# Attention layers: inverse sums applied to the weighted values of a head group instead of to the probabilities

## The chip, the core and the metric

The kernel runs on one core of a Trainium2 chip. Its engines are TensorE (PE; PEld is its weight load), VectorE (DVE), ScalarE (ACT), GpSimd (POOL) and SyncE (SP), which issues DMAs. The metric is the device time in microseconds of one execution, as the median of several runs.

## The reference

Four layers in a row on x of 4 x 512 x 512, all in float32. Layer 0 is attention with 16 heads of 32, normalized queries and keys, and an MLP; layer 1 is attention with a sparse causal mask, 16 heads of 32 and 4 key heads; layer 2 is attention with 8 heads of 64 on one key head, and a gated MLP; layer 3 is a set of small experts. What the change touches is in all three attentions (layer 0 shown; x grows by the result times gamma1):

```python
scores = jnp.einsum('bhqd,bhkd->bhqk', qn, kn) + attn_bias
p = jax.nn.softmax(scores, axis=-1)
o = jnp.einsum('bhqk,bhkd->bhqd', p, v)
o = jnp.transpose(o, (0, 2, 1, 3)).reshape(Bs, Lx, Cx)
return o @ Wproj.T + bproj
```

## The kernel before

One function, `attention`, builds the three attention layers (tags l0a, l1a, l2a), each as a block in which every engine has its own program. The batches (4) are the outer loop. A batch is cut into head groups of four heads (`NG` = 4 groups in layers 0 and 1, 2 in layer 2; `NO` accumulators psO of 128 rows each, 1 or 2), a head group into four tiles of 128 queries (`NT`), and a query tile into its four heads. So a head group has 16 steps, one for each pair of query tile and head, a batch 64 (layer 2: 32), and a quarter of a head group is four steps. The order is written out by hand: `steps` gives each engine, for step n, the same list of side jobs.

For the tile of step n:

- TensorE computes its scores (`scores`, 128 queries by up to 512 keys; 128 or 198 in layer 1) two steps ahead in layer 0, one step ahead in layers 1 and 2, into one of `NS` = 3 banks (layer 2: 2).
- VectorE adds the mask and takes the minimum of the negated scores (`minima`, L1095), which writes the tile to `prob`.
- ScalarE takes the exponential and the row's sum (`exps`, L837; sums in `ssum`).
- After four tiles, behind the minimum of the next one, VectorE makes the four inverse sums in one reciprocal (`inverse_sums`, L1102, of 128x4), and GpSimd multiplies the four tiles with them (L1259 and L1261) and counts `p_done`.
- Six steps after its own step (`LAG`), TensorE transposes the tile (`transposes`, L673, one transpose for each 128 keys). ScalarE copies three of four to `PT`, VectorE the fourth (L1110).
- `weigh` (L695) multiplies four such tiles with the values, into `psO`, which gathers a whole head group transposed: row 32j + d (or 64j + d) is column d of head j, the free axis is the 512 queries. The last one of a group is in step 7 of the next.
- In step 7 ScalarE copies `psO` to the high part `oTh` (`o_copy`, L855), in step 8 VectorE makes the remainder `oTl` (`o_rest`, L1117). Both add the value bias in layer 0. The output projection (`out`, L588) of a batch runs in the next one, as four side jobs at the steps `OUT_AT`, each with a residual on VectorE.

The other side jobs of TensorE all write one of two banks `psA`, in turn: the query and key projections of layer 0 (steps 2, 4, 6 and 9), its value projections (7 and 8), transposes of the normalized rows, and from step 12 to 15 those of the next group's queries and keys. VectorE prepares the next group meanwhile (`prepare`): in layer 0 squares and sums (steps 1 and 2), three steps of an inverse square root on 128x32 (steps 3 to 5, the helper at L82, L84 and L86), the scaling (6), and the split into stacked parts (9, 11, 13 and 14); in layers 1 and 2 rotations and stacks.

In layer 0 GpSimd also adds the projected bias `bG` to the four residual tiles, one in each of the last four quarters of a batch (L1267). SP loads `G` and `bG` for a batch after the residuals of the one before.

Of the kernel before, what the change touches and what calls it, by code (L numbers as in the profile page):

```python
# [25 lines left out]
P = 128  # L26
# [234 lines left out]
def attention(nc, R, D, L, scale_g, shift_g):  # L261
# [28 lines left out]
    with ExitStack() as ctx:  # L290
# [38 lines left out]
        rinv = S.sb("rinv", [P, NP])  # L329
# [4 lines left out]
        if is0:  # L334
            qb = S.sb("qb", [P, C])
            G = S.sb("G", [P, C])
            bG = S.sb("bG", [P, C])
            nrm = S.sb("nrm", [P, 4, 4 * 8])
            sq = xn[:].rearrange("p r c -> p (r c)").rearrange("p (t w) -> p t w", w=QKW)
# [17 lines left out]
        if is2:  # L357
# [19 lines left out]
        s_done, min_done, exp_done, rinv_done, p_done = (  # L377
            S.sem(n) for n in ("s_done", "min_done", "exp_done", "rinv_done", "p_done"))
# [17 lines left out]
        OUT_AT = (9, 10, 11, 20) if is0 else (12, 13, 14, 15)  # L396
# [17 lines left out]
        def jobs(n, first, more):  # L414
# [3 lines left out]
            todo = []  # L418
            if hg < NG:
# [41 lines left out]
        def banked(first, more, last):  # L461

            n_, out = 0, []
# [15 lines left out]
        with nc.Block() as block:  # L479

            @block.sync
            def _(sp):
# [29 lines left out]
            def _(pe):  # L512
# [79 lines left out]
                def run(job, i, b, bn, bo):  # L592
# [72 lines left out]
                def transposes(b, m, first):  # L665
# [3 lines left out]
                    pe.wait_ge(p_done, b * NTILE + (m + 1))  # L669
# [6 lines left out]
                def weigh(b, u, first):  # L676
# [53 lines left out]
            def _(act):  # L730
# [118 lines left out]
                def o_copy(b, hg):  # L849

                    act.wait_ge(pv_done, b * U + (hg + 1) * NT)
                    for o in range(NO):
                        k = hg % NG * NO + o
                        bias = R.vb[:, k:k + 1] if is0 else R.zero[:]
                        act.activation(oTh[:, k, :], psO[o][:], ACT.Identity, bias=bias).then_inc(oh_done, 1)  # L855

                def batch(b, first, more):
                    for n, _, todo, m in steps(first, more):
# [8 lines left out]
                        if n % GS == LAG + 1 and n <= NTILE + LAG + 1 and not (first and n == LAG + 1):  # L867
# [34 lines left out]
            def _(v):  # L902
# [62 lines left out]
                if is0:  # L965
                    qk_tiles = (nrm[:, 1, :], nrm[:, 0, :], nrm[:, 2, :], nrm[:, 3, :].bitcast(I32))
# [132 lines left out]
                def inverse_sums(b, u):  # L1099
# [996 lines left out]
```

## Time and profile before

| | us |
|---|---|
| median of 3 runs | 2933.84 (2933.4 to 2935.29) |
| the profiled execution | 2936.59 |
| its span, first to last instruction | 2934.8 |
| TensorE busy | 2468.2 (84%) |
| VectorE busy | 1624.5 (55%) |
| ScalarE busy | 1207.7 (41%) |
| GpSimd busy | 907.7 (31%) |

The mean granted clock of TensorE over the span is 0.89 of full speed. The score loops of the attention layers begin at 101, 1243 and 1735 us of the span and end at 760, 1652 and 2088. An MLP stands between the first two, layer 2's MLP and the experts behind the last. Busy time is a sum over the engine's instructions and does not tell whether somebody waited for them.

### The profile page before, as it was taken

To read this page: it belongs to the slowest core of one execution; us is meant where nothing else is said; L and a number is where in the kernel's file an instruction comes from. 1 tells how busy PE (TensorE), PEld (TensorE's weight loads), DVE (VectorE), ACT (ScalarE), POOL (GpSimd) and SP (SyncE) were. 2 spreads that over 40 slices of the span, in tenths; PEclk is the share of its full clock that TensorE was granted. 3 is DMA by queue.
4 is the path that set the end of the run, shared out by engine and by line. 5 is a ranking of instruction groups with operands and counts; after the bars stand their busy time and mean duration, and the time that the engine had idled before them with its cause. 6 is when DMAs were issued, how large, how long until landed. Compare 5 with 4: busy or idle time off the path is not lost. (4 is left out here: it accounts for less than half of the span.)

```text
span 2934.8 us, 48110 instructions
## 1 busy us (share of the span) xinstructions
PE 2468.2 (84%) x15828; PEld 2016.5 (69%) x15828; DVE 1624.5 (55%) x4635; ACT 1207.7 (41%) x2980; POOL 907.7 (31%) x982
## 2 busy tenths in 40 slices
PE   5879789798589999688788758889789999996786
PEld 4767677677468888576656547767568888885565
DVE  2677766677664343465575466576453333333876
ACT  1565565556441111365665546555431111112442
POOL 0133333233366676232232213233211212120422
PEclk8899889799889999768778779989989999997898
DMA  5000000000200000100000000000100000001000
GB/s 205 23 1 2 9 2 9 1 2 9 75 27 18 26 29 0 70 30 1 2 1 1 2 33 1 1 0 1 44 22 22 35 31 21 0 0 47 1 29 29
DMA packets 15743, 63.12 MB, mean 22 GB/s; under 512 B 2588, under 2 KB 3356, under 8 KB 10548
## 3 DMA queue, kind: packets, MB, share of 16 engines
q1 hardware_dynamic: 15540, 60.59, 5.8%
q8 instruction: 105, 1.72, 0.2%
q14 instruction: 98, 0.80, 0.1%
HBM read 56.36 MB, written 4.23 MB: 21 GB/s over the span
## 5 line engine op out<-in xcount | busy, mean ns | idle before, releaser
L837 ACT ACTIVATE l0a_prob<-l0a_prob,l0a_nmin 128x512 f32<-128x512 f32 x256 | 185.7, 725 | 199.5 <-DVE l0a_nmin L1095 199.2
L1617 POOL TENSOR_TENSOR l2m_hidl<-l2m_hid,l2m_hidh 128x512 fp32r<-128x512 f32 x64 | 100.9, 1576 | 480.2 <-DVE l2m_hidh L1593 480.2
L1259 POOL TENSOR_TENSOR l0a_prob<-l0a_prob,l0a_rinv 128x512 f32<-128x512 f32 x64 | 66.6, 1040 | 533.1 <-DVE l0a_rinv L1102 533.1
L1485 ACT ACTIVATE l2m_gate<-l2m_psG 128x512 f32<-128x512 f32 x64 | 38.3, 598 | 452.0 <-PE l2m_psU L1426 452.0
L1588 DVE TENSOR_TENSOR l2m_hid<-l2m_gate,l2m_psU 128x512 f32<-128x512 f32 x64 | 44.0, 688 | 300.1 <-ACT l2m_gate L1485 300.1
L673 PE MATMUL l0a_psT<-res_ident,l0a_prob 128*128 128x128 f32 x1024 | 165.9, 287 | 11.8 <-ACT l0a_PT L847 11.7
L1095 DVE CUSTOM_DVE_ANT_0 l0a_prob<-l0a_psS,l0a_mask 128x512 f32<-128x512 f32 x256 | 173.2, 687 | 2.6 <-issue 1.6
L1636 POOL TENSOR_TENSOR res_X<-res_X,l0m_share 128x512 f32<-128x512 f32 x128 | 162.1, 1293 | 25.7 <-DVE l0m_share L1577 24.7
L535 PE MATMUL l0a_psA<-l0a_wh,l0a_hTh 128*128 128x128 f32 (+1 forms) x512 | 155.5, 304 | 11.2 <-DVE l0a_wl L1210 5.8
L651 PE MATMUL l0a_psS<-l0a_kT,l0a_qT 96*128 96x512 f32 x256 | 128.0, 502 | 43.2 <-DVE l0a_nmin L1095 28.3
L1489 ACT ACTIVATE l0m_hid<-l0m_psG,l0m_b1c 128x512 f32<-128x512 f32 x64 | 44.0, 690 | 287.5 <-PE l0m_psG L1426 284.3
L673 PEld LDWEIGHTS l0a_psT<-res_ident,l0a_prob 128*128 128x128 f32 x1024 | 133.6, 147 | 38.6 <-ACT l0a_PT L847 19.0
L535 PE MATMUL l0a_psA<-l0a_wl,l0a_hTh 128*128 128x128 f32 (+1 forms) x512 | 149.2, 291 | 0.0
L535 PE MATMUL l0a_psA<-l0a_wh,l0a_hTl 128*128 128x128 f32 (+1 forms) x512 | 148.8, 291 | 0.0
L1261 POOL TENSOR_SCALAR l0a_prob<-l0a_prob,l0a_rinv 128x512 f32<-128x512 f32 x192 | 145.2, 772 | 0.0
L673 PE MATMUL l1a_psT<-res_ident,l1a_prob 128*128 128x128 f32 x448 | 120.5, 351 | 29.1 <-ACT l1a_PT L847 26.3
L837 ACT ACTIVATE l1a_prob<-l1a_prob,l1a_nmin 128x198 f32<-128x198 f32 (+1 forms) x256 | 114.6, 449 | 68.7 <-DVE l1a_nmin L1095 67.7
L1259 POOL TENSOR_TENSOR l1a_prob<-l1a_prob,l1a_rinv 128x128 f32<-128x128 f32 (+1 forms) x64 | 32.3, 505 | 338.4 <-DVE l1a_rinv L1102 338.4
L1259 POOL TENSOR_TENSOR l2a_prob<-l2a_prob,l2a_rinv 128x512 f32<-128x512 f32 x32 | 33.7, 1054 | 324.6 <-DVE l2a_rinv L1102 324.6
L847 ACT ACTIVATE l0a_PT<-l0a_psT 128x512 f32<-128x512 f32 x192 | 113.1, 595 | 41.7 <-PE l0a_psO L695 28.2
L837 ACT ACTIVATE l2a_prob<-l2a_prob,l2a_nmin 128x512 f32<-128x512 f32 x128 | 92.6, 724 | 87.5 <-DVE l2a_nmin L1095 87.2
L1593 DVE CAST l0m_hidh<-l0m_hid 128x512 fp32r<-128x512 f32 x64 | 33.0, 515 | 160.9 <-ACT l0m_hid L1489 160.9
(390 smaller groups left out, 7875.3 us busy)
## 6 DMA issues: line engine op xcount, KB each, us to landing
l2m_stage<-in_l2m_w SPq DMA_DIRECT2D x8, 1536.0 KB, 6.6
l0m_stage<-in_l0m_w SPq DMA_DIRECT2D x8, 1024.0 KB, 4.8
cond_w<-in_wmod SPq DMA_DIRECT2D x6, 1024.0 KB, 5.9
res_X<-in_x SPq DMA_DIRECT2D x4, 1024.0 KB, 11.9
l0a_prob<-in_l0a_w SPq DMA_DIRECT2D x4, 1024.0 KB, 6.6
l1a_wmod<-in_wmod SPq DMA_DIRECT2D x4, 1024.0 KB, 5.4
out<-res_X SPq DMA_DIRECT2D x4, 1024.0 KB, 4.3
l_stage<-in_l_w SPq DMA_DIRECT2D x3, 1024.0 KB, 7.2
```

Source lines behind the costliest of these rows:

```text
L535: mm = pe.matmul(ps[:, c0:c0 + n], l[:, k, t * P:(t + 1) * P], cols(r, k), start=(k == 0 and i == 0), stop=(k == NK - 1 and i == 2))
L651: mm = pe.matmul(out, q, kT[:, j, 0:w], start=True, stop=True)
L673: mm = pe.transpose(psT[m % 2][:, c * P:(c + 1) * P], prob[:, m % NP, k0:k0 + P], R.ident[:])
L837: act.activation(prob[:, n % NP, 0:w], src[:, 0:w], ACT.Exp, bias=nmin[:, n % NP:n % NP + 1], scale=-1.0, accum_out=ssum[:, n % NP:n % NP ...
L847: act.activation(PT[:, j, 0:w], psT[m % 2][:, 0:w], ACT.Copy).then_inc(pT_act, 1)
L1095: v.tensor_tensor_reduce(prob[:, n % NP, 0:w], psS[s_bank(n)][:, 0:w], other, -L.scale, BIG, ALU.add, ALU.min, nmin[:, n % NP:n % NP + 1]) ...
L1259: op = pool.tensor_tensor(x, x, r.to_broadcast([P, w]), ALU.mult)
L1261: op = pool.tensor_scalar(x, x, r, 1.0, ALU.mult, ALU.mult)
L1489: act.activation(hid[:, m, :], psG[m][:], ACT.Gelu_apprx_tanh, bias=b1c[:, par * MT + m:par * MT + m + 1]).then_inc(act_done, 1)
L1588: v.tensor_tensor(hid[:, m, :], gate[:, m, :], psU[m][:], ALU.mult).then_inc(hid_done, 1)
L1617: pool.tensor_tensor(hidl[:, s % 2, m, :], hid[:, m, :], f32(hidh[:, s % 2, m, :]), ALU.subtract).then_inc(hl_done, 1)
L1636: pool.tensor_tensor(x, x, share[:, t, :], ALU.add).then_inc(x_done, 1)
```

## The change

The probabilities are left undivided. `inverse_sums` writes the reciprocal of each sum once for every column of its head, so that four heads fill the 128 columns of an accumulator's row order: 128 elements per query tile in layers 0 and 1, and 2x128 in layer 2. After each second query tile TensorE transposes two such tiles in a side job "rT" (at step 9 for the first half of a group, at step 2 of the next group for the second half; 2 x NO transposes of 128x128 in a job, waiting on `rinv_done`), and ScalarE copies the result to `rT`. In step 7 VectorE multiplies `psO` with `rT` in place (`o_scale`, NO operations of 128x512). ScalarE's `o_copy` and VectorE's `o_rest` read `rT` instead of `psO` and move from steps 7 and 8 to 8 and 9. Transposes of probabilities wait for `exp_done` instead of `p_done`; the weighing of a new group waits for `on_done`.

GpSimd keeps only layer 0's additions of the bias, four in a row once the last head group has begun. `bG` is gone: `G` holds the bias row first and the gain row after the additions. Layer 0's output jobs move from steps 9, 10, 11 and 20 to 10, 11, 19 and 21.

```diff
-        rinv = S.sb("rinv", [P, NP])
+        rinv = S.sb("rinv", [P, 2, NO, P])
+        rT = S.sb("rT", [P, NO, T])
...
-        OUT_AT = (9, 10, 11, 20) if is0 else (12, 13, 14, 15)
+        OUT_AT = (10, 11, 19, 21) if is0 else (12, 13, 14, 15)
+        RT_AT = {9: (0, 0), 2: (-1, 1)}
...
+            if s in RT_AT and n <= NTILE + 2 and not (first and n == 2):
+                todo.append(("rT", hg + RT_AT[s][0], RT_AT[s][1]))
...
+                        sp.dma_start(G[:], bcast_rows(D["gam_rows"][1, b])).then_inc(g_in, 16)
+                        sp.wait_ge(xg_done, b + 1)
                         sp.dma_start(G[:], bcast_rows(D["gam_rows"][0, b])).then_inc(g_in, 16)
-                        sp.dma_start(bG[:], bcast_rows(D["gam_rows"][1, b])).then_inc(g_in, 16)
...
+                    elif kind == "rT":
+                        pe.wait_ge(rinv_done, 2 * g + x + 1)
+                        for o in range(NO):
+                            for t in range(2):
+                                c0 = (2 * o + t) * P
+                                mm = pe.transpose(psA[i][:, c0:c0 + P], rinv[:, t, o, :], R.ident[:])
+                        mm.then_inc(rT_mm, 1)
+                        freed[i] = [(rT_done, 2 * g + (x + 1))]
...
-                    pe.wait_ge(p_done, b * NTILE + (m + 1))
+                    pe.wait_ge(exp_done, b * NTILE + (m + 1))
...
-                        pe.wait_ge(oh_done, b * NG * NO + u // NT * NO)
-                        pe.wait_ge(ol_done, b * NG * NO + u // NT * NO)
+                        pe.wait_ge(on_done, b * NG * NO + u // NT * NO)
...
+                    elif kind == "rT":
+                        act.wait_ge(rT_mm, 2 * g + (x + 1))
+                        if x == 0:
+                            act.wait_ge(ol_done, NO * g)
+                        act.activation(rT[:, :, x * 2 * P:(x + 1) * 2 * P],
+                                       psA[i][:, 0:NO * 2 * P].rearrange("p (o q) -> p o q", o=NO),
+                                       ACT.Copy).then_inc(rT_done, 1)
...
-                        act.activation(oTh[:, k, :], psO[o][:], ACT.Identity, bias=bias).then_inc(oh_done, 1)
+                        act.activation(oTh[:, k, :], rT[:, o, :], ACT.Identity, bias=bias).then_inc(oh_done, 1)
...
-                    v.reciprocal(rinv[:, s0:s0 + 4], ssum[:, s0:s0 + 4]).then_inc(rinv_done, 1)
+                    if u % 2 == 0 and not (first and u < 2):
+                        v.wait_ge(rT_mm, b * 2 * NG + u // 2)
+                    sums = ssum[:, s0:s0 + 4].rearrange("p (o j) -> p o j", o=NO)[:, :, :, None]
+                    inv = v.reciprocal(rinv[:, u % 2].rearrange("p o (j d) -> p o j d", d=HD),
+                                       sums.to_broadcast([P, NO, 4 // NO, HD]))
+                    if u % 2 == 1:
+                        inv.then_inc(rinv_done, 1)
...
+                def o_scale(b, hg):
+                    v.wait_ge(pv_done, b * U + (hg + 1) * NT)
+                    v.wait_ge(rT_done, 2 * (b * NG + hg + 1))
+                    for o in range(NO):
+                        v.tensor_tensor(rT[:, o, :], psO[o][:], rT[:, o, :], ALU.mult).then_inc(on_done, 1)
...
-                        v.scalar_tensor_tensor(oTl[:, k, :], psO[o][:], bias, f32(oTh[:, k, :]), ALU.add,
+                        v.scalar_tensor_tensor(oTl[:, k, :], rT[:, o, :], bias, f32(oTh[:, k, :]), ALU.add,
...
-                            if j == 0:
-                                op = pool.tensor_tensor(x, x, r.to_broadcast([P, w]), ALU.mult)
-                            else:
-                                op = pool.tensor_scalar(x, x, r, 1.0, ALU.mult, ALU.mult)
-                            op.then_inc(p_done, 1)
...
+                    with pool.Fori(0, B) as b:
+                        pool.wait_ge(rinv_done, 2 * (b * NG + NG - 1))
+                        pool.wait_ge(g_in, 32 * b + 16)
+                        for t in range(NT):
+                            x = R.X[:, bass.ds(b * NT + t, 1), :].rearrange("p o c -> p (o c)")
+                            add = pool.tensor_tensor(x, x, G[:], ALU.add)
+                        add.then_inc(xg_done, 1)
```

## Rows read from the trace of the kernel before

**Rows 1.** Busy us by engine, the score loops of the three attention layers

```profile
core 0: us, PE busy (x) PEld busy (x) DVE busy (x) ACT busy (x) POOL busy (x), PEclk, DMA share, GB/s
101.00:760.00 659.00, 556.19 (x5308) 470.18 (x5308) 471.98 (x1469) 400.24 (x968) 225.96 (x267) 0.91 0.02 4
1243.00:1652.00 409.00, 345.69 (x2419) 265.33 (x2421) 245.82 (x1323) 262.15 (x1002) 122.05 (x252) 0.76 0.02 6
1735.00:2088.00 353.00, 305.14 (x2333) 253.21 (x2334) 226.48 (x684) 206.19 (x488) 110.22 (x124) 0.92 0.00 1
```

**Rows 2.** Waits of TensorE in layers 0 and 1: us in total, times, longest

```profile
PE l0a_psS L651 <- DVE l0a_nmin L1095: 28.3, 25, 2.4
...
PE l1a_psT L673 <- POOL l1a_prob L1259: 1.8, 1, 1.8
```

**Rows 3.** By source line, layer 1, four elements: ns min/median/max

```profile
L1102 DVE RECIPROCAL l1a_rinv<-l1a_ssum x64: 165/173/180, 1248.0 to 1652.6; 128x4 f32<-128x4 f32 x64
...
L911 DVE COPY l1a_mod<-res_M x4: 145/145/152, 1203.2 to 1520.2; 128x4 f32<-128x4 f32 x2, 128x4 f32 x2
...
L923 DVE TENSOR_SCALAR l1a_rs<-l1a_mv x4: 169/170/171, 1204.0 to 1521.0; 128x4 f32<-128x4 f32 x4
```

**Rows 4.** Busy us, layer 1, batch 1, quarters of head groups, as rows 1

```profile
1359.90:1363.70 3.80, 2.76 (x30) 1.89 (x28) 3.36 (x17) 3.04 (x13) 2.06 (x4) 1.00 0.02 4
...
1367.20:1382.50 15.30, 14.40 (x80) 11.15 (x78) 5.69 (x30) 5.79 (x23) 1.95 (x4) 0.82 0.00 0
...
1388.30:1392.10 3.80, 2.85 (x31) 1.97 (x29) 3.37 (x18) 3.26 (x15) 2.06 (x4) 1.00 0.01 2
...
1434.80:1445.50 10.70, 10.70 (x71) 8.62 (x69) 1.60 (x15) 4.74 (x16) 1.75 (x4) 1.00 0.01 2
```

**Rows 5.** Busy time, layer 2, batch 1, two quarters

```profile
1843.00:1855.30 12.30, 8.91 (x80) 7.43 (x78) 10.94 (x32) 9.63 (x26) 3.19 (x4) 0.97 0.00 1
...
1873.60:1890.60 17.00, 17.00 (x110) 14.00 (x109) 4.14 (x15) 7.05 (x16) 3.06 (x4) 1.00 0.00 1
```

**Rows 6.** Busy time, layer 0, batch 1, two quarters (278.7 is step 8)

```profile
270.50:278.70 8.20, 7.26 (x80) 6.47 (x80) 7.22 (x21) 4.25 (x11) 3.05 (x4) 1.00 0.01 2
278.70:294.30 15.60, 15.60 (x133) 13.84 (x132) 9.01 (x29) 7.55 (x19) 3.20 (x4) 1.00 0.00 1
```

**Rows 7.** Timeline of VectorE and GpSimd, layer 0: start us, us, engine, line

```profile
354.50 0.19 DVE L84 SCALAR_TENSOR_TENSOR l0a_nrm<-l0a_nrm 128x32 f32<-128x32 f32 x1
...
356.63 1.04 POOL L1259 TENSOR_TENSOR l0a_prob<-l0a_prob,l0a_rinv 128x512 f32<-128x512 f32 x1 [10.64 <-DVE l0a_rinv L1102]
356.70 1.02 DVE L84 SCALAR_TENSOR_TENSOR l0a_nrm<-l0a_nrm 128x32 f32<-128x32 f32 x1
```

**Rows 8.** Groups of VectorE's instructions, layers 0 and 2: busy us, mean ns

```profile
L84 DVE SCALAR_TENSOR_TENSOR l0a_nrm<-l0a_nrm 128x32 f32<-128x32 f32 x45 | 18.6, 413 | 3.4
...
L86 DVE SCALAR_TENSOR_TENSOR l0a_nrm<-l0a_nrm 128x32 f32<-128x32 f32 x45 | 13.4, 297 | 3.3
...
L82 DVE TENSOR_TENSOR l0a_nrm<-l0a_nrm 128x32 f32<-128x32 f32 x45 | 11.2, 249 | 0.0
...
L1044 DVE TENSOR_TENSOR l2a_stack<-l2a_raw,l2a_stack 128x256 fp32r<-128x256 f32 x28 | 18.0, 642 | 2.1
...
L1044 DVE TENSOR_TENSOR l2a_stack<-l2a_raw,l2a_stack x32: 424/426/1151, 1731.0 to 2054.9; 128x256 fp32r<-128x256 f32 x32
```

**Rows 9.** Layer 0's timeline, tail and loop, and ScalarE's copies of 128x256

```profile
772.58 0.69 DVE L1126 TENSOR_TENSOR l0a_xn<-l0a_psA,l0a_G 128x512 f32<-128x512 f32 x1 [3.11 <-PE l0a_psA L588]
...
775.30 0.69 DVE L1126 TENSOR_TENSOR l0a_xn<-l0a_psA,l0a_G 128x512 f32<-128x512 f32 x1 [1.26 <-PE l0a_psA L588]
...
351.50 0.60 PE L673 MATMUL l0a_psT<-res_ident,l0a_prob 128*128 128x128 f32 x4
...
L813 ACT ACTIVATE l0a_V<-l0a_psA 128x256 f32<-128x256 f32 x30 | 11.6, 387 | 17.5 <-PE l0a_psA L535 17.5
```

**Rows 10.** Timeline of GpSimd, layer 0, last batch: an addition of the bias

```profile
748.85 1.29 POOL L1267 TENSOR_TENSOR res_X<-res_X,l0a_bG 128x512 f32 x1
```

More of the change, by code:

```diff
@@ L336, in attention @@
             G = S.sb("G", [P, C])
-            bG = S.sb("bG", [P, C])
-            nrm = S.sb("nrm", [P, 4, 4 * 8])
+            nrm = S.sb("nrm", [P, 3, 4 * 8])
             sq = xn[:].rearrange("p r c -> p (r c)").rearrange("p (t w) -> p t w", w=QKW)
@@ L376, in attention @@
         qT_mm, kT_mm, qT_done, kT_done = (S.sem(n) for n in ("qT_mm", "kT_mm", "qT_done", "kT_done"))
-        s_done, min_done, exp_done, rinv_done, p_done = (
-            S.sem(n) for n in ("s_done", "min_done", "exp_done", "rinv_done", "p_done"))
+        s_done, min_done, exp_done, rinv_done = (
+            S.sem(n) for n in ("s_done", "min_done", "exp_done", "rinv_done"))
+        rT_mm, rT_done, on_done = (S.sem(n) for n in ("rT_mm", "rT_done", "on_done"))
         pT_mm, pT_act, pT_dve, pv_done, oh_done, ol_done = (
@@ L461, in banked @@
         def banked(first, more, last):
-            n_, out = 0, []
+            n_, out = int(first), []
             for n in range(NTILE + (OUT_AT[-1] + 2 if last else 0)):
@@ L866, in batch @@
                             pT_copy(b, m - CL, first)
-                        if n % GS == LAG + 1 and n <= NTILE + LAG + 1 and not (first and n == LAG + 1):
+                        if n % GS == LAG + 2 and n <= NTILE + LAG + 2 and not (first and n == LAG + 2):
                             o_copy(b, n // GS - 1)
@@ L965, in _ @@
                 if is0:
-                    qk_tiles = (nrm[:, 1, :], nrm[:, 0, :], nrm[:, 2, :], nrm[:, 3, :].bitcast(I32))
+                    qk_tiles = (nrm[:, 1, :], nrm[:, 0, :], nrm[:, 2, :], nrm[:, 2, :].bitcast(I32))
                 def qk_norms():
@@ L1097, in minima, with inverse_sums @@
                                            nmin[:, n % NP:n % NP + 1]).then_inc(min_done, 1)
-                def inverse_sums(b, u):
+                def inverse_sums(b, u, first):
                     v.wait_ge(exp_done, b * NTILE + (4 * u + 4))
                     s0 = 4 * u % NP
-                    v.reciprocal(rinv[:, s0:s0 + 4], ssum[:, s0:s0 + 4]).then_inc(rinv_done, 1)
+                    if u % 2 == 0 and not (first and u < 2):
[5 more added lines that the diff above has]
+                        inv.then_inc(rinv_done, 1)
                 def pT_copy(b, m, first):
@@ L1124, in residual @@
                         if t == 0:
-                            v.wait_ge(xg_done, bo + 1)
+                            v.wait_ge(g_in, 32 * (bo + 1))
                         v.tensor_tensor(xn[:, t % XS, :], ps[:], G[:], ALU.mult)
@@ L1168, in batch @@
                         if n % 4 == 0 and n <= NTILE and not (first and n == 0):
-                            inverse_sums(b, n // 4 - 1)
+                            inverse_sums(b, n // 4 - 1, first)
                         if hg < NG and (more or hg < NG - 1):
@@ L1185, in batch @@
                                 norm_rows(b + 1, NORM_T.index(s - NORM0 + 1))
-                        if s == LAG + 2 and n <= NTILE + LAG + 2 and not (first and n == LAG + 2):
+                        if s == LAG + 1 and n <= NTILE + LAG + 1 and not (first and n == LAG + 1):
+                            o_scale(b, hg - 1)
+                        if s == LAG + 3 and n <= NTILE + LAG + 3 and not (first and n == LAG + 3):
                             o_rest(b, hg - 1)
@@ L1250, in _ @@
             def _(pool):
-                def batch(b):
-                    for u in range(U):
-                        pool.wait_ge(rinv_done, b * U + (u + 1))
-                        w = L.width[u % NT]
-                        for j in range(4):
-                            s = (4 * u + j) % NP
-                            x, r = prob[:, s, 0:w], rinv[:, s:s + 1]
-                            if j == 0:
-                                op = pool.tensor_tensor(x, x, r.to_broadcast([P, w]), ALU.mult)
-                            else:
-                                op = pool.tensor_scalar(x, x, r, 1.0, ALU.mult, ALU.mult)
-                            op.then_inc(p_done, 1)
-                        if is0 and u >= U - 4:
-                            if u == U - 4:
-                                pool.wait_ge(g_in, 32 * (b + 1))
-                            x = R.X[:, b * NT + (u - (U - 4)), :]
-                            add = pool.tensor_tensor(x, x, bG[:], ALU.add)
-                            if u == U - 1:
-                                add.then_inc(xg_done, 1)
-                with pool.Fori(0, B) as b:
-                    batch(b)
+                if is0:
+                    with pool.Fori(0, B) as b:
[5 more added lines that the diff above has]
+                        add.then_inc(xg_done, 1)
         S.close()
```

2 lines of the change are left out of this document (1 added, 1 removed).

## Prediction

> **What bounds the kernel now.** I read the busy time by stage first, cutting the span at the first and the last score of each attention layer. The three layers' loops take 659, 409 and 353 of 2934.8 us; nothing else in the program is touched. In all three TensorE is busy 84 to 86% of the time, VectorE 60 to 72%, ScalarE 58 to 64%, GpSimd 30 to 34% [rows 1]. GpSimd has the most room of all, and the waits say the same: the largest entry of TensorE waiting for a GpSimd product is 1.8 us, once, against 28.3 us for VectorE's minima in layer 0 [rows 2]. So the removed work was not the end of a path by itself; its latency (a group of four tiles) is hidden, because a tile is transposed six steps after its score.
>
> An average over a layer hides who binds. Scores run only one or two tiles ahead of the minima, so TensorE, VectorE and ScalarE are locked together within about two steps. I therefore cut batch 1 of each layer into quarters of a head group (four tiles, starting at steps 0, 4, 8 and 12) and read each engine's busy time. Some quarters are full on VectorE (3.36 of 3.8 us, 3.37 of 3.8), others are full on TensorE while VectorE stands idle (10.70 of 10.7 us against 1.60) [rows 4]. Layer 2 shows both kinds [rows 5], layer 0 too [rows 6]. What is added to VectorE costs its length in the first kind and nothing in the second.
>
> My rule is: a quarter counts whole if VectorE is busy 85% of it, half from 68 to 84%, else nothing. Layer 0: 2 whole and 8 half of 16, so 6. Layer 1: 7 whole and 3 half, so 8.5. Layer 2, with 8 quarters: 4 whole and 1 half, so 4.5. Over four batches that is 24 of 64, 34 of 64 and 18 of 32 quarters.
>
> **1. The reciprocals grow.** This is the term that decides. Each quarter has one, right behind the minimum of its first tile. Now it makes 4 elements in 173 to 174 ns; after the change it writes each inverse sum once per column of the head: 4x32 = 128 elements in layers 0 and 1, 4x64 = 256 in layer 2. No row shows a long reciprocal, so I bound its rate from short ones. Lower bound: a scalar operation on 4 elements takes 170 ns [rows 3], so 3 ns more, and one element per clock as the 512-wide operations show: 128 elements then cost 0.13 us more than 4, and 256 cost 0.26 more. Upper bound: a copy of 4 elements takes 145 ns [rows 3]. If the reciprocal has the copy's fixed part, 28 ns more are due to four elements, 7 ns each, and about 8 with the 1 ns that the copy needs itself. Then 128 elements cost 124 x 8 = 0.99 us more, and 256 cost 252 x 8 = 2.02 us more. I take the upper value: both are plain operations with one input and no scalar operand, and the copy is the nearer relative. With the quarters above: layer 0 24 x 0.99 = 24, layer 1 34 x 0.99 = 34, layer 2 18 x 2.02 = 36, together 94 us. At the lower rate it is 3 + 4 + 5 = 12.
>
> The Trainium skill ("VectorE: DVE Perf Modes", section "Walkthrough: the 8-slice pipeline in each mode") says that the reciprocal is an iterative divide on two slices with a repeat count of 8. It gives no time per element; read as eight clocks for each it would agree with the upper bound, and read as a pipeline depth alone it would leave the lower one. That reading speaks against this change.
>
> **2. GpSimd's multiplications go, and with them its hold on VectorE.** A step of the inverse square root takes 0.19 us, but 1.02 us where GpSimd's product runs [rows 7]. Over layer 0's loop the three lines of that step average 413, 297 and 249 ns (45 times each) [rows 8]; against 190 undisturbed [rows 7] that is 10.0 + 4.8 + 2.7 = 17.5 us, in steps 3 to 5, where the minima are what TensorE waits for. I count it whole. Stacks, casts and scaling in the same layer show perhaps 25 us more by the same subtraction, mostly beside full TensorE; I count 4.5 of them. Layer 2: the stack's subtraction averages 642 against 426 ns, 28 times, so 6 us, and I count 7 with its casts. Layer 1's columns are short; 3 us. Total -32.
>
> **3. VectorE multiplies the weighted values** (line added as o_scale, step 7). One 128x512 product of PSUM and SBUF takes 0.69 us [rows 9]; 16 of them in layers 0 and 1 each, 16 in layer 2 (two per head group). It waits for the last weighing of the group, and behind it stand the minimum of step 8, and through that the exponential and a score. In layer 0 TensorE is full there with the value projections [rows 6], so 0. In layer 1 three of four step-7 quarters are VectorE's: 12 x 0.69 = 8. In layer 2 about three of four: 12 x 0.69 = 8. The copy to the high part and the remainder move one step later each and now read SBUF; I cost that at nothing while the steps 8 and 9 keep their length; if not, it is the same 0.7 us per group. The accumulator of weighted values comes free earlier, which nobody waits for.
>
> **4. Small transposes and their copies.** 64 transposes per layer. Four of them in a row take 0.60 us, of which the last one's latency is 0.27, so 0.11 us apiece [rows 9]: 7 us per layer at the upper clock, twice that at the lower. Those of step 2 often meet a waiting TensorE. Half in layer 0: 4. In layer 1, at a granted clock of 0.76 [rows 1], 5. In layer 2, 3. The copies by ScalarE: 32 of 128x256 in layers 0 and 1 (0.39 us [rows 9]) and 16 of 128x512 in layer 2, 10 to 12 us per layer; ScalarE is idle over a third of the time, and I count 0, 3 and 3. New waits: the first transposes of a group wait at step 9 for the reciprocal of step 8, with the projection of that step behind them; their copy waits for the remainder of the group before (VectorE, step 9), with the next exponential behind it. That exponential needs the minimum of step 10, which VectorE makes later anyway. So 0 beyond what is counted.
>
> **5. Layer 0's bias rows and the output projection.** The four additions of the bias (1.29 us each [rows 10]) were spread over the last four quarters and now run in one burst at the start of the last group, beside VectorE's squares: +2. SP loads the gain row behind them instead of beside the bias; it is needed at step 10 of the next batch, most of a 41 us head group later (659 us over 16 groups), so 0. One output tile per batch, 2.72 us of TensorE (from one residual product to the next [rows 9]), moves out of the full steps 9 to 11 to steps 19 and 21, where TensorE waits; its two VectorE operations go with it. 3 x (2.7 - 1.4) = -4.
>
> **6. The tails.** After the last score nothing else covers: one product of 0.69 us, a handover, and a long reciprocal. +2, +2, +3.
>
> **Sum.** Layer 0: 24 - 22 + 0 + 4 + 2 - 4 + 2 = +6. Layer 1: 34 - 3 + 8 + 8 + 2 = +49. Layer 2: 36 - 7 + 8 + 6 + 3 = +46. Together +101 on the profiled execution's 2936.6 us, which lies 2.8 us above the median of the three runs. On the median's scale: 2933.8 + 101 = 3034.8, so **3035 us**. Counting only whole quarters, the reciprocals give 68 instead of 94: 3009. Counting twice the half ones gives 3061; all 160 exposed (127 + 65 = 191) would be 3132, which the full TensorE quarters exclude.
>
> **Rivals.**
> - **A cheap reciprocal.** Term 1 is 12, the rest stays: +19, 2953 us. For it: the scalar operation's 170 ns. Against: the copy's 145 ns. Chance 0.20.
> - **Relief wins, faster than before.** GpSimd's hold is all on the path: 42 us in layer 0, 5 in layer 1 and 12 in layer 2, 27 more than I count, so all but the reciprocals comes to +7 - 27 = -20. This decides if 128 elements cost less than 0.21 us more than 4 (20/94 of 0.99), that is under 1.7 ns each. At the lower rate: -20 + 12 = -8, 2926 us; with the copies hidden too, 2915. Against: the disturbed stacks lie beside a full TensorE. Chance 0.11.
> - **The long reciprocals are covered.** TensorE's 84% means that it takes the next place at once: half of term 1, 47 us, so 2934 + 7 + 47 = 2988 us. For it: TensorE full in many quarters [rows 4 to 6]. Against: VectorE full in as many. Chance 0.14.
> - **The clock falls with it.** Layer 1 already has a granted clock of 0.76 against 0.91 and 0.92 [rows 1]; longer gaps could put more of it at 1.2 instead of 2.4 GHz. Were layer 1 at 0.65, its 346 us of TensorE work grow by some 40 us, most of it shown: 3070 us. Chance 0.10.
> - **My forecast**, 0.45, with its own range 3005 to 3065.
>
> **Chances and range.** This kernel's runs can tell 0.2%, 6 us. Faster by more: the relief rival without its upper part, 0.10. Within: the rest of it and the near side of the cheap reciprocal, 0.06. Slower: 0.84. The range is 2942 to 3085: it leaves out the faster cases, some of the cheap case and the far end of the clock's case.
>
> **What would show it.** The row of the reciprocals: 1.1 to 1.2 us for 128 elements, 2.1 to 2.2 for 256 (0.30 and 0.43 by the lower rate). The three root lines back at about 190 ns. VectorE's busy time up by some 200 us in all (160 reciprocals: 127 + 65, products 33, relief -50), and its quarters that were full before longer by the reciprocal, with TensorE waiting for minima more often. TensorE's quarters of full load unchanged. Layer 0 nearly level, layers 1 and 2 longer by 10%. I am wrong if the reciprocal is short, or if layers 1 and 2 keep their length with a long one.

## The result and the profile after

| | before | after |
|---|---|---|
| median | 2934.57 us (4 runs, 2933.4 to 2940.08) | 3014.23 us (4 runs, 2998.81 to 3021.22) |
| ratio | | 1.0269, 95% interval 1.0236 to 1.0302 |
| span of the profiled execution | 2934.8 us | 3010.9 us |

The changed kernel is slower by 2.7%. I forecast 3035 us, 21 us more than it takes. The head of the profile after, busy us and share by engine:

```profile
PE 2521.7 (84%) x16020; PEld 2056.0 (68%) x16020; DVE 1735.3 (58%) x4683; ACT 1242.7 (41%) x3060; POOL 460.5 (15%) x342
```

VectorE has 111 us more work where I forecast 200 (the parts that I gave for it, 127 + 65 + 33 - 50, make 175), GpSimd 447 less. The stages, as in rows 1 (columns: the stretch, its length, busy us of PE, PEld, DVE, ACT and POOL, granted clock, DMA share and GB/s; from the first to the last minimum of each layer):

```profile
101.10:764.40 663.30, 571.65 (x5345) 484.22 (x5347) 482.70 (x1480) 409.53 (x995) 19.98 (x16) 0.90 0.02 4
1253.10:1695.70 442.60, 362.74 (x2466) 277.58 (x2469) 295.65 (x1336) 273.84 (x1029) 0.00 (x0) 0.73 0.02 6
1780.30:2159.90 379.60, 317.38 (x2374) 259.79 (x2373) 268.70 (x695) 214.35 (x499) 0.00 (x0) 0.92 0.00 1
```

The same cut of the kernel before, its 256, 256 and 128 minima:

```profile
101.90:758.80 656.90, 554.12 (x5283) 468.59 (x5285) 471.25 (x1467) 398.32 (x964) 224.76 (x266) 0.91 0.02 4
1244.30:1651.50 407.20, 344.08 (x2404) 263.89 (x2407) 245.45 (x1321) 260.71 (x998) 122.05 (x252) 0.76 0.02 6
1736.00:2087.50 351.50, 303.64 (x2320) 251.90 (x2321) 225.98 (x681) 204.87 (x484) 109.73 (x124) 0.92 0.00 1
```

I call the length from the first to the last minimum of a layer its loop. The loops grew by 6.4, 35.4 and 28.1 us: 70 of the 76 us between the two spans. The other 6 lie in the tails and starts of the layers. The reciprocals (columns of this view: count, ns min/median/max, first and last start), against rows 3:

```profile
L1124 DVE RECIPROCAL l0a_rinv<-l0a_ssum x64: 945/948/954, 109.3 to 766.1; 128x128 f32<-128x128 f32 x64
L1124 DVE RECIPROCAL l1a_rinv<-l1a_ssum x64: 946/948/954, 1256.8 to 1696.8; 128x128 f32<-128x128 f32 x64
L1124 DVE RECIPROCAL l2a_rinv<-l2a_ssum x32: 1746/1748/1753, 1786.3 to 2161.6; 128x256 f32<-128x256 f32 x32
```

They grew by 0.775 us (948 less 173 ns) and 1.575 us (1748 less 173): 6.25 ns for each added element, where I took 8. The lines of the inverse square root are back where they are undisturbed (against rows 8; busy us, mean ns, idle before), and the product costs what I took:

```profile
L86 DVE SCALAR_TENSOR_TENSOR l0a_nrm<-l0a_nrm 128x32 f32<-128x32 f32 x45 | 8.7, 193 | 3.3
L84 DVE SCALAR_TENSOR_TENSOR l0a_nrm<-l0a_nrm 128x32 f32<-128x32 f32 x45 | 8.7, 193 | 4.1 <-issue 0.9
L82 DVE TENSOR_TENSOR l0a_nrm<-l0a_nrm 128x32 f32<-128x32 f32 x45 | 7.7, 172 | 0.0
...
L1141 DVE TENSOR_TENSOR l0a_rT<-l0a_psO,l0a_rT 128x512 f32<-128x512 f32 x15 | 10.3, 688 | 2.6 <-PE l0a_psO L707 2.5
```

Among the waits (us in total, times, longest) two are new, TensorE's small transposes for the reciprocals and, in layer 0, the output projection for the copy of an inverse:

```profile
PE l0a_psS L664 <- DVE l0a_nmin L1114: 17.4, 17, 2.4
...
PE l1a_psA L615 <- DVE l1a_rinv L1124: 12.7, 13, 1.6
...
PE l0a_psA L593 <- ACT l0a_rT L821: 6.3, 6, 2.0
```

The first of the three was 28.3 us [rows 2]: TensorE waits less for layer 0's minima than before. That fits a relief, and doesn't show where it went. Of the third's 6.3 us, 5.7 are three waits, one in each of layer 0's groups 5, 9 and 13: the output job at step 19 takes the bank of the small transposes of step 18 and waits for ScalarE's copy out of it.

### The profile page after: what moved, and what is told of

Same layout as the page of the kernel before. It is cut to its first block and busy times, and to the rows that moved or that the text cites. A ratio compares the mean times of both kernels' runs of the same rounds, so it can differ in the third digit from the quotient of the medians.

```text
span 3010.9 us, 48062 instructions
## 1 busy us (share of the span) xinstructions
PE 2521.7 (84%) x16020; PEld 2056.0 (68%) x16020; DVE 1735.3 (58%) x4683; ACT 1242.7 (41%) x3060; POOL 460.5 (15%) x342
## 5 line engine op out<-in xcount | busy, mean ns | idle before, releaser
L540 PE MATMUL l0a_psA<-l0a_wh,l0a_hTh 128*128 128x128 f32 (+1 forms) x512 | 157.2, 307 | 8.9 <-DVE l0a_wl L1243 5.8
L1290 POOL TENSOR_TENSOR res_X<-res_X,l0a_G 128x512 f32 x16 | 20.0, 1281 | 726.4 <-DVE l0a_rinv L1124 726.4
L1114 DVE CUSTOM_DVE_ANT_0 l2a_prob<-l2a_psS,res_zero 128x512 f32<-128x512 f32 x128 | 87.4, 687 | 51.3 <-issue 50.8
L540 PEld LDWEIGHTS l0a_psA<-l0a_wh,l0a_hTh 128*128 128x128 f32 x512 | 106.5, 208 | 12.1 <-DVE l0a_wl L1243 6.2
L1114 DVE CUSTOM_DVE_ANT_0 l1a_prob<-l1a_psS,l1a_mask 128x198 f32<-128x198 f32 (+1 forms) x256 | 85.3, 341 | 45.8 <-issue 45.5
```

The source lines that it names most:

```text
L540: mm = pe.matmul(ps[:, c0:c0 + n], l[:, k, t * P:(t + 1) * P], cols(r, k), start=(k == 0 and i == 0), stop=(k == NK - 1 and i == 2))
L1114: v.tensor_tensor_reduce(prob[:, n % NP, 0:w], psS[s_bank(n)][:, 0:w], other, -L.scale, BIG, ALU.add, ALU.min, nmin[:, n % NP:n % NP + 1]) ...
```

## The experiments

**The way to read them.** Each kernel takes the change apart by one more step, so that the differences add up to it: before, e1 (no products), e2 (long reciprocals), e5 (the moved steps), e4 (small transposes and copies), after (the product). The loops below are in us, each from the kernel's one profiled execution; each ratio is to runs of before on the same chip. Head groups are counted from 0 through the four batches, 16 in layer 0.

| | layer 0: its 13 plain groups + groups 2, 6, 10 | layer 1 | layer 2 | median | ratio to before, interval |
|---|---|---|---|---|---|
| before | 498.8 + 158.1 | 407.2 | 351.5 | 2934.6 | |
| e1 | 486.2 + 147.0 | 401.3 | 347.8 | 2907.2 | 0.991 (0.9875 to 0.9946) |
| e2 | 492.0 + 151.6 | 422.7 | 368.7 | 2953.7 | 1.0069 (1.0044 to 1.0093) |
| e3 | 509.9 + 160.5 | 426.3 | 379.3 | 2994.9 | 1.0212 (1.0175 to 1.025) |
| e9 | 491.6 + 155.3 | 422.7 | 368.7 | 2960.4 | 1.0109 (1.0088 to 1.0129) |
| e5 | 491.6 + 159.9 | 430.2 | 371.6 | 2970.8 | 1.0131 (1.0111 to 1.015) |
| e4 | 498.2 + 157.2 | 435.5 | 376.2 | 2988.0 | 1.0184 (1.0147 to 1.0221) |
| after | 505.8 + 157.5 | 442.6 | 379.6 | 3014.2 | 1.0269 (1.0236 to 1.0302) |
| e7 | 492.9 + 154.7 | 435.2 | 364.8 | 2972.6 | 1.0139 (1.0119 to 1.016) |
| e8 | 491.5 + 146.6 | 430.0 | 362.3 | 2966.5 | 1.0118 (1.0099 to 1.0138) |
| e6 | 494.9 + 149.6 | 407.5 | 351.4 | 2922.4 | 0.9979 (0.9962 to 0.9996) |
| e10 | 501.7 + 149.2 | 404.5 | 351.5 | 2929.4 | 1.0008 (0.9994 to 1.0021) |
| e11 | 491.9 + 146.5 | 404.3 | 351.5 | 2924.0 | 0.9976 (0.9964 to 0.9988) |
| e12 | 511.2 + 169.0 | 407.6 | 354.4 | 2966.8 | 1.011 (1.0087 to 1.0134) |

Layer 0's groups 2, 6 and 10 (those in which the next batch is normalized) stand apart because they take one of several lengths in the same kernel; the section "What the clock does" below is on that. Group 14 stands among the plain ones, but in after it had the same trouble, and that is in its 505.8. Layers 1 and 2 repeat well: kernels that have the same work there agree within 0.1 us in layer 2 except e12, and within 3.3 in layer 1.

### e1: no products

```diff
-                            op = pool.tensor_tensor(x, x, r.to_broadcast([P, w]), ALU.mult)
...
-                    pe.wait_ge(p_done, b * NTILE + (m + 1))
+                    pe.wait_ge(exp_done, b * NTILE + (m + 1))
```

> The kernel before with GpSimd's multiplications of the probabilities left out (the output projection works on undivided probabilities; nothing takes their place). It shows the relief by itself. The sum's theory: the three root lines fall from 413, 297 and 249 ns to about 190, 190 and 170, and the time falls by 32 us to about 2902 us: the first to the last minimum of layer 0 takes 635 us (657 before), layer 1 404 (407 before), layer 2 345 (352 before). The relief rival: all of the hold was on the path, 59 us less, 2875 us, layer 0 at 615. A third theory, that VectorE's shorter instructions only wait longer for TensorE: the root lines fall all the same, but the time by 10 us at most, layer 0 at 647 or more.

Measured: 2907.2 us, 0.9% less than before; the loops are shorter by 23.7, 5.9 and 3.7 us. The relief term (22, 3, 7) holds in sum and nearly by layer; by the medians it is 28 us. The relief rival (2875) and the third theory (10 us at most) are both out. In the mean time from each minimum to the next, layer 0 gains 1.10 us at step 4, where the inverse square root stood, and loses 0.22 at step 5. But only 12.6 of layer 0's 23.7 us are in the 13 plain groups; 11.1 are in groups 2, 6 and 10, and 5 of these are a third quarter at a higher granted clock (see below).

### e2 and e3: the long reciprocals alone

```diff
-                    v.reciprocal(rinv[:, s0:s0 + 4], ssum[:, s0:s0 + 4]).then_inc(rinv_done, 1)
+                    v.reciprocal(rinv[:, s0:s0 + 4, :], ssum[:, s0:s0 + 4, None].to_broadcast([P, 4, HD])).then_inc(rinv_done, 1)
```

> As e1_no_products, but each reciprocal writes its inverse sums once per column of the head, as in the changed kernel: 128 elements in layers 0 and 1, 256 in layer 2 (nobody reads them). Nothing else is added, so against e1 it shows the long reciprocals alone. The sum's theory with the measured growth of 0.775 and 1.575 us and my 24, 34 and 18 exposed quarters: 73 us over e1, about 19 in layer 0, 26 in layer 1, 28 in layer 2. The rival of covered reciprocals: half, 37 us. All 160 exposed would be 150 us.

> The kernel before, whole, with the long reciprocals; GpSimd multiplies as before with the first column of each head. Against the kernel before it shows the long reciprocals beside GpSimd's products. The sum's theory: 73 us, 3007 us. If the covered rival holds, 37 us, 2971. If relief and long reciprocals draw on the same slack (the reciprocal fills what the products' hold leaves), e3 minus before and e2 minus e1 differ by over 10 us; if the terms add, they agree within 10.

In e2, e3 and e9 the inverse square root of layer 0 also has three small buffers instead of four, as in the changed kernel; no run has that alone.

Measured: e2 is 46.5 us above e1 by the medians (e1's profiled execution was its fastest, 9 us below its median), by the loops 10.4 + 21.4 + 20.9 = 53. Both lie between the two theories (73 and 37): the size was known by then, so it is my count of exposed quarters that is too high. The steps tell which. Mean time from minimum n to the next, e2 less e1:

| step | 0 | 1 | 4 | 5 | 8 | 9 | 12 | 13 |
|---|---|---|---|---|---|---|---|---|
| layer 0 | +0.09 | 0 | +0.75 | -0.32 | +0.19 | -0.12 | +0.19 | -0.02 |
| layer 1 | +0.28 | -0.19 | +0.61 | -0.03 | +0.66 | -0.12 | +0.73 | -0.53 |
| layer 2 | +0.51 | -0.13 | +0.93 | -0.09 | +1.53 | -0.24 | +1.29 | -1.44 |

A reciprocal delays the minimum behind it. At steps 4 and 8 of layers 1 and 2 most of that stays; at 12 most or all of it is given back within one step, where TensorE makes the next group's queries and keys. In layer 0 it is mainly the one at step 4 that stays. So of four reciprocals about two bind in layers 1 and 2 and one in layer 0. Counting my whole quarters alone, at the measured size, gives 53 us (8 x 0.775 + 28 x 0.775 + 16 x 1.575), the same as the loops, by layer 6, 22 and 25 against 10, 21 and 21. Layer 1's granted clock is 0.73 in e2 against 0.76 in e1, so a part of the price may be paid through the clock; no run separates that.

e3 costs 60 us by the loops (13.5, 19.1, 27.8) and 59 by the medians. Against e2 less e1 that is 8 us more by the loops and 13 by the medians, on both sides of the 10 that I had set. So the terms nearly add; the part that doesn't is in layer 2, +6.9, and what makes it isn't known.

### e5 and e9: the moved steps

e5 is e4 (below) with the small transposes, their copies and the waits on them left out; e9 is e2 with layer 0's output jobs moved:

```diff
-        OUT_AT = (9, 10, 11, 20) if is0 else (12, 13, 14, 15)
+        OUT_AT = (10, 11, 19, 21) if is0 else (12, 13, 14, 15)
```

> As e4_after_no_scale, and the small transposes of the inverse sums with ScalarE's copies of them left out too. What stays of the change: products gone, long reciprocals, high part and remainder one step later, the output jobs and the bias additions of layer 0 moved. e4 minus this is the transposes' and copies' price: the sum has 4 in layer 0, 8 in layer 1, 6 in layer 2. This minus e2_no_products_long (2954 us) is the price of the moves: the sum has -2, all in layer 0. By e4 and e2 the two together cost 32 us, twice the sum, 12 of them in layer 0. If the transposes are the cause: this kernel at 2952, e4 32 to 36 above it. If layer 0's moves are: this kernel at about 2963, with layer 0 at 653 (e2: 644).

> e2_no_products_long with layer 0's output jobs moved as in the changed kernel. It splits layer 0's moves. e6 showed that this move alone takes layer 0 from 657 to 644 in the kernel before. If the gain stays without GpSimd's products, layer 0 is at 631 here (e2: 644, so the whole at 2941), and the later high part and remainder cost layer 0 the rest up to e5's 651.5: 20 us, more than one 0.75 us remainder in each of 16 groups (12). If the relief and the move draw on the same slack in steps 3 to 5, layer 0 stays at 644 and the later remainder costs 8, as in layer 1.

Measured: e5 at 2970.8 and its layer 0 at 651.5: neither theory alone. In layers 1 and 2 two things lie between e2 and e5: the high part and the remainder come one step later, and VectorE still waits in step 7 for the last weighing of the group, as it does in the changed kernel before its product. Together they cost 7.5 and 2.9 us; no run separates them. I had the move at nothing. The steps say that the wait is small in layer 1 (step 7 is 0.04 us longer) and may be a large part in layer 2 (0.22 us in each of 8 groups). The remainder leaves step 8 and enters step 9 (layer 1: -0.56 and +0.88 us a step; layer 2: -1.13 and +1.37), so step 8 gives back less than step 9 costs. In layer 0 the shift is alike (-0.77 and +0.88), and the 13 plain groups come out level, 491.6 in e9 and e5; the 4.6 us between their loops are all in groups 2, 6 and 10.

e9 was expected at 631 in layer 0 if the output jobs' move kept e6's gain. It has 646.9, and in the plain groups 491.6 against e2's 492.0: with the long reciprocals and without products the move is worth nothing there. That the two draw on the same slack is my second reading in the expectation; no run separates it further.

### e4: without the product of the weighted values

```diff
-                    for o in range(NO):
-                        v.tensor_tensor(rT[:, o, :], psO[o][:], rT[:, o, :], ALU.mult).then_inc(on_done, 1)
...
-                        act.activation(oTh[:, k, :], rT[:, o, :], ACT.Identity, bias=bias).then_inc(oh_done, 1)
+                        act.activation(oTh[:, k, :], psO[o][:], ACT.Identity, bias=bias).then_inc(oh_done, 1)
```

> The changed kernel without VectorE's multiplication of the weighted values (o_scale; it still waits for the copies, and the high part and the remainder read the accumulator undivided). Against the changed kernel (3014 us; first to last minimum 663, 443 and 380 us) it shows that product alone. The sum's theory: 16 us less, 0 in layer 0, 8 in layer 1, 8 in layer 2, 2998 us. If it is covered everywhere: within 5 us. If its handover from TensorE and to ScalarE costs more than its length: over 25 us, with layer 0 shorter as well.

Measured: 2988.0, 26 us below after by the medians and 18.4 by the loops (7.9, 7.1, 3.4). In layers 1 and 2 step 7 is 0.38 and 0.46 us longer with the product, and that stays. In layer 0 it is 0.48 us longer and the steps 8 and 9 give it back in nearly every group; 7.1 of layer 0's 7.9 us lie in group 14 alone, and 6.6 of these in one step. That is not VectorE's product but TensorE's clock. The quarters from step 4 and from step 8 of group 14 in after (columns as in the stages above):

```profile
709.90:718.10 8.20, 7.22 (x52) 5.53 (x52) 7.11 (x22) 4.46 (x11) 0.00 (x0) 0.50 0.00 1
718.10:734.00 15.90, 15.90 (x99) 14.86 (x97) 6.38 (x22) 6.11 (x16) 0.00 (x0) 0.52 0.01 2
```

And in e4:

```profile
708.80:716.50 7.70, 6.95 (x52) 5.29 (x53) 6.54 (x21) 4.09 (x11) 0.00 (x0) 0.56 0.00 1
716.50:726.20 9.70, 9.70 (x105) 8.90 (x103) 6.51 (x25) 6.47 (x16) 0.00 (x0) 1.00 0.01 3
```

Without group 14 the product costs layer 0 0.8 us, which is the 0 of the sum. Whether the product made the clock come back late there isn't shown: of after's four executions three have a mean clock of 0.878 to 0.880, and the fourth, at 0.887 like e4's four (0.887 to 0.888), takes 2998.8 us, 11 us above e4's median.

e4 less e5 is the price of the small transposes and copies: 6.6 us in layer 0's plain groups (3.9 in the whole loop), 5.3 and 4.6 in the others; the sum had 4, 8 and 6. In layer 0 it lies in groups 5, 9 and 13 (2.6, 2.6 and 2.0 us), where the output job waits for ScalarE's copy out of its bank, and I had put such waits at 0.

### e7 and e8: short reciprocals, then spread

```diff
-                    inv = v.reciprocal(rinv[:, u % 2].rearrange("p o (j d) -> p o j d", d=HD),
-                                       sums.to_broadcast([P, NO, 4 // NO, HD]))
+                    v.reciprocal(inv4[:], ssum[:, s0:s0 + 4])
+                    v.drain()
+                    few = inv4[:].rearrange("p (o j) -> p o j", o=NO)[:, :, :, None]
+                    inv = v.tensor_copy(rinv[:, u % 2].rearrange("p o (j d) -> p o j d", d=HD),
+                                        few.to_broadcast([P, NO, 4 // NO, HD]))
```

> The changed kernel, whole, with the reciprocal back at 4 elements (0.17 us) and a copy by VectorE that spreads it to 128 or 256 columns. The copy moves one element per clock: I expect 0.2 us for 128 and 0.35 for 256, so each inverse grows by some 0.25 and 0.4 us instead of 0.775 and 1.575. With e2 minus e1 (10, 21 and 21 us in the three layers for the long ones) the sum's theory gives back two thirds in layers 0 and 1 and three quarters in layer 2: 36 us, 2978. If the clock or the new waits and not the reciprocals make the changed kernel slow: within 10 us of 3014.

In e8 the second step is GpSimd's: `pool.tensor_tensor(rinv, few, zero, ALU.add)`.

> The changed kernel, whole, with the reciprocal of 4 elements on VectorE and the spreading on GpSimd, which is idle, as a sum with zero of 128 or 256 elements (the bias additions of layer 0 stand behind them, one for each of four quarters). The reciprocals then cost VectorE what they did before. The sum's theory: all of e2 minus e1 comes back, 52 us of the loops, less up to 0.4 us for each first transposes of a group at step 9, which wait for one more engine (40 groups, so 0 to 16 us): 2962 to 2978. It is faster than e7 if VectorE is what ends there, slower if the latency is.

Measured: 2972.6 and 2966.5 us. Both do the whole work of the changed kernel, and they give back 42 and 48 us by the medians. By the loops it is 38 and 55 us, but 6 and 14 of these are four third quarters of layer 0 (groups 2, 6, 10 and 14), whose granted clocks differ. What is left, and the layers 1 and 2 by themselves (22 and 30 us), is over half of the 53 us that the reciprocals took. So the reciprocals are the largest single cause, and the rival in which the clock or the new waits carry the change falls. VectorE's copy takes (busy us, mean ns)

```profile
L1127 DVE COPY l0a_rinv<-l0a_inv 128x128 f32<-128x128 f32 x64 | 14.5, 227 | 4.7
```

for 128 elements, and GpSimd's sum 0.40 us (0.29 and 0.61 for layer 2's 256). e8 has the waits that I feared: in layer 1 step 8 is 0.72 us shorter than in after, and step 9 is 0.57 longer. That step has the small transposes, and TensorE waits 10.5 us in 13 places of layer 1 for GpSimd's sum. It still wins over e7 by 6 us.

### e6 and e10: layer 0's output jobs in the kernel before

```diff
-        OUT_AT = (9, 10, 11, 20) if is0 else (12, 13, 14, 15)
+        OUT_AT = (10, 11, 19, 21) if is0 else (12, 13, 14, 15)
```

e10 has (19, 20, 21, 22) in the same place.

> The kernel before with one edit, layer 0's output jobs at steps 10, 11, 19 and 21. The sum's theory: 3 x (2.7 - 1.4) = 4 us less, all in layer 0, 0.14%, at the edge of what can be told. If the steps 19 and 21 have no free TensorE: no change in the time, and the steps after 19 and 21 longer by what 9 to 11 lose. If the output's VectorE operations meet full VectorE quarters there: up to 3 x 1.4 = 4 us more.

> The kernel before with all four of layer 0's output jobs at steps 19 to 22 (before: 9, 10, 11 and 20). e6 gained 12 us in layer 0 from one job more in this stretch and none at step 9. If TensorE's full steps 9 to 11 are what ends there, two more jobs out of them give up to 2 x 3 x 2.7 = 16 us more than e6: layer 0 at 630 to 640. If steps 19 to 22 have no room left, or the residuals on VectorE fill its minima's time there: 645 or more.

Measured: e6 0.9979 (0.9962 to 0.9996), layer 0's plain groups 3.9 us shorter: the 4 us of the sum. Groups 2, 6 and 10 are 8.5 us shorter, nearly all of it third quarters at a higher granted clock (12.2 us each at 1.00). e10 gives nothing (1.0008); its plain groups are 2.9 us longer than before, and what each batch's first group gains (8 to 9 us) the second one loses again. So steps 19 to 22 had room for one job more, not for three.

### e11 and e12: a version that uses this

e11 takes e8's layer 0 and leaves layers 1 and 2 as they were before; e12 moves its first small transposes:

```diff
-        RT_AT = {9: (0, 0), 2: (-1, 1)} if is0 else {}
+        RT_AT = {12: (0, 0), 2: (-1, 1)} if is0 else {}
```

> Layer 0 as in e8_short_pool (weighted values scaled, 4-element reciprocals spread by GpSimd, output jobs moved), layers 1 and 2 as in the kernel before, where the change costs 14 to 23 us even with short reciprocals. By the loops of e8 and before: layer 0 at 638 (657 before), layer 1 at 407, layer 2 at 352, so 17 to 19 us less than before, 2915 us, ratio 0.994. e6_before_out_moved has 644 in layer 0, so the scaling would be worth 6 us there.

> As e11_hybrid (2924 us; layer 0 at 638.5), with the first small transposes of a group moved from step 9, where TensorE is full in layer 0, to step 12; GpSimd's spreading for the third query tile waits for them instead. In e11 steps 7 to 11 take 12.0 us a group against 11.5 in e6, which has no small transposes. If the two transposes at step 9 are that half microsecond, layer 0 loses 0.3 to 0.5 us in each of 16 groups: 630 to 634, time 2917. If steps 12 to 15 are as full, 638 again. The groups 2, 6 and 10 of layer 0 stay at 49 us each, unless the granted clock comes back late there (up to 5 us each).

Measured: e11 at 2924.0 us, ratio 0.9976 (0.9964 to 0.9988). It beats both kernels, by 0.24% and 3%, but so does e6 with one line: the scaling gains nothing over e6 that these runs tell. The loops are those expected (638.5, 404.3, 351.5), the gain in time is smaller, 6 us by the medians where I wrote 17 to 19: I had compared with one profiled execution of before whose groups 2, 6 and 10 were slow.

e12 is a miss: 2966.8 us where 2917 was expected. The small transposes at step 12 share two banks with the queries' and keys' transposes, which now wait for ScalarE's copy. TensorE's waits in e12, of which the second isn't among those of e11 at this line:

```profile
PE l0a_psA L588 <- ACT l0a_qT L858: 23.0, 23, 3.1
PE l0a_psA L588 <- ACT l0a_rT L829: 21.9, 15, 1.7
```

Step 13 grew from 2.95 to 4.83 us. And groups 2, 6 and 10 lost 22.5 us, 12.8 of them in the third quarter (steps 8 to 12), to which nothing was added; the next section is on that.

## What the clock does

In layer 0's groups 2, 6 and 10 the second quarter (steps 4 to 8) has little for TensorE, and its granted clock there is 0.50 to 0.63 of full speed, so 1.2 GHz for all or most of it. What the next quarter takes depends on when 2.4 GHz comes back. Two neighbouring quarters in three kernels, as rows 4. Group 10 before:

```profile
535.30:549.20 13.90, 8.58 (x60) 6.66 (x60) 11.70 (x46) 3.68 (x9) 3.04 (x4) 0.54 0.01 2
549.20:566.70 17.50, 17.50 (x113) 16.54 (x113) 9.36 (x28) 9.23 (x25) 3.19 (x4) 0.59 0.01 1
```

The same group in e1, without products:

```profile
522.80:535.50 12.70, 8.59 (x65) 6.65 (x66) 10.50 (x46) 3.68 (x9) 0.00 (x0) 0.60 0.01 2
535.50:547.70 12.20, 10.87 (x112) 9.74 (x111) 8.80 (x28) 9.04 (x25) 0.00 (x0) 1.00 0.01 2
```

And in after:

```profile
534.20:548.20 14.00, 9.11 (x62) 7.19 (x63) 11.80 (x46) 4.52 (x12) 0.00 (x0) 0.54 0.00 1
548.20:565.30 17.10, 17.10 (x113) 16.19 (x112) 9.50 (x28) 8.99 (x23) 0.00 (x0) 0.58 0.00 1
```

The same 112 or 113 matmuls keep TensorE busy for 10.9 or 17.5 us. Over the first 13 kernels' traces (39 such quarters) I found three kinds: 21 take 12.2 to 12.9 us at a clock of 1.00, 12 take 15.0 to 16.1 at 0.78 to 0.81, 6 take 17.1 to 17.7 at 0.57 to 0.60. Groups 6 and 10 are the same code in the same execution and differ (before: 15.0 and 17.5). e8 and e11 have all three fast, e12 has 17.2, 17.1 and 15.4. So about 5 us for each of three groups can come or go with an edit elsewhere, and a single profile's layer 0 is only good to about that. It is why the table keeps these groups apart. Group 14, which after has at 0.52 and 15.9 us, takes 8.4 to 10.9 us at 0.93 or more in the same quarter of all the other kernels. What decides which kind a group gets isn't settled: a short second quarter isn't enough (12.5 us in e1's group 2 was followed by 15.3) and a long one is no hindrance (14.5 in e3 by 12.2).

## Why the prediction was right, and where it was off

The sign, the range and the main cause were right; the value was 21 us too high, and that it came so near is in part luck, as below. By its own steps:

| term of the sum | forecast, layers 0/1/2 | measured by the loops | from |
|---|---|---|---|
| 1 long reciprocals | +24/+34/+36 | +10.4/+21.4/+20.9 | e2 less e1 |
| 2 relief | -22/-3/-7 | -23.7/-5.9/-3.7 | e1 less before |
| 3 product of the weighted values | 0/+8/+8 | +7.9/+7.1/+3.4 | after less e4 |
| 3 high part and remainder later, with the wait in step 7 | 0/0/0 | +4.6/+7.5/+2.9 | e5 less e9 (layer 0), less e2 |
| 4 small transposes and copies | +4/+8/+6 | +3.9/+5.3/+4.6 | e4 less e5 |
| 5 output jobs and bias | -2 | +3.3 | e9 less e2; the bias is in the row of e5 |
| 6 tails | +7 | +6 | the spans less the loops |
| sum | +101 | +76 | |

In layer 0 this table mixes the kernel with the clock. Of its rows in the plain groups alone the relief is -12.6, the reciprocals +5.8, the product +0.5 without group 14 (which has 7.1), the later remainder 0, the small transposes +6.6 and the output jobs -0.4.

- **Term 1** is where it was off, by 41 us. First its size: 8 ns an element by the copy's fixed part [rows 3], in truth 6.25. At the right size my own count of quarters gives 24 x 0.775 + 34 x 0.775 + 18 x 1.575 = 73. Then its exposure: 53. The rule "85% busy counts whole, 68 to 84% half" looked at a quarter's average; the steps show that the reciprocal of step 12 is given back one step later. The whole quarters alone make the 53.
- The choice between the bounds was right: the copy's fixed part was the nearer relative. The sentence of the Trainium skill's page "VectorE: DVE Perf Modes" (section "Walkthrough: the 8-slice pipeline in each mode") on an iterative divide with a repeat count of 8 points the same way; read as eight clocks for each element it would stand at my upper bound of 0.99 us more, and the trace has 0.775: it pointed to the right bound, and eight clocks for each element is not what was measured.
- **Term 2** came out in size, -33 against -32 by the loops and -28 by the medians. A third of it (11 us) is in groups 2, 6 and 10, 5 us of that a matter of when the clock came back, which I didn't foresee.
- **Term 3** put layer 0's product at nothing behind a full TensorE, and that holds: 0.8 us, the rest of the row is the clock in group 14. Layer 2's was half of what I took. The later remainder was costed at nothing with "the same 0.7 us per group" as the alternative: layer 1 pays 0.47 a group.
- **Term 4** was near in size and wrong in kind for layer 0: the cost stands in three groups, where an output job waits for a copy out of its bank (5.7 us in all), and the prediction counted new waits as 0.
- **Term 5**: e6 confirms 4 us for the output jobs in the kernel before; with the long reciprocals and without the products (e9) they are worth nothing in the plain groups. That relief and this move help at the same steps is a reading, not shown.
- Errors of both signs met: 41 us too much in term 1, 17 too little in terms 2 to 5 (15 of them the later remainder), 1 in the tails. Term 1 alone would have left the forecast 41 us too high; that the others brought it within 21 is luck, as the largest of them is a cost that I had put at nothing. The clock's parts in groups 2, 6 and 10 cancel over the rows (their third quarters take 44.8 us before and 44.7 after), those of group 14 don't (+5.0).
- **The rivals.** The cheap reciprocal falls by its row. Relief does not win, as the reciprocals cost more than 1.7 ns an element and 53 us in all. "Covered" was near in its own term (47 us where 53 were measured), and short by the terms that I had too low: it gave 2988 us. The clock rival was put in layer 1 (0.76 to 0.65); layer 1 has 0.73. In layer 0 the clock made 5.0 of the 6.4 us by which that loop grew (the third quarter of group 14, 10.9 us before and 15.9 after).
- Of the signs: layers 1 and 2 longer by 8.7% and 8.0% (forecast 10), layer 0 by 1% (nearly level), VectorE busy +111 (200 said, 175 by its parts): the reciprocals 139 (e2 less e1, all loops), the product 33 (48 of 0.69), the relief -59 (e1 less before, where I had 50).

## What to carry over

Before an operation is widened to save one elsewhere, find its time per element on that engine: written 128 wide a reciprocal takes 0.95 us, a copy 0.23, and four elements followed by a spread of 0.23 us did the same work here for 42 us less. Count the exposure of an added operation step by step rather than by the busy share of a quarter; what the next step gives back doesn't count. And take a change apart so that its pieces add up: here pieces from 3 to 53 us, of both signs, stood behind one number that looked like a good forecast. Then look whether a difference is spread over the groups or sits in one of them: layer 0's 7.9 us for the product were one quarter at a lower clock.

## What the runs showed of the hardware

- A reciprocal on VectorE, in float32 on 128 rows, takes 6.25 ns more for each element of a row: 0.173 us for 4, 0.948 for 128, 1.748 for 256. A copy to 128 elements takes 0.227.
- VectorE's operations on SBUF that overlapped GpSimd's products took up to 1.02 us instead of 0.19 [rows 7]; without the products the three lines in layer 0 (45 each) average 172 to 193 ns.
- After a quarter at a granted clock of 0.50 to 0.63 TensorE did the next quarter's work in 12.2 to 12.9 us at 1.00, in 15.0 to 16.1 at 0.78 to 0.81 or in 17.1 to 17.7 at 0.57 to 0.60, with the same code, even in one execution. In group 14 of after it was busy all through 15.9 us at 0.52.
